# A fused expert MLP and adapter kernel: the order of its front and its drain, and the down projection from f16 parts

## The reference, cut to what matters

```python
# layer 0, expert e = itok_B_0_7[b]
h = gelu(x @ Wi[e] + bi[e])                  # 256 -> 1024
r = h @ Wo[e] + bo[e] + x                    # 1024 -> 256
y = (r - mean) * rsqrt(var + 1e-12) * gamma[e] + beta[e]
# layer 1, domain d = itok_B_0_15[b]
a = gelu(y @ down_W.T + down_b)              # 256 -> 64, the "down projection"
a = a @ expert_W[d].T + expert_b[d] + domain_emb[d]
r = a @ up_W.T + up_b + y                    # 64 -> 256
out = (r - mean) * rsqrt(var + 1e-5) * ln_gamma + ln_beta
```

## Time and profile before

| what | value |
|---|---|
| median of the runs | 487.38 us |
| the profiled execution: time and span | 487.38 us, 485.6 us |
| mean granted TensorE clock | 0.981 |
| PE busy | 457.4 us (94%) |
| DVE, ACT, POOL busy | 341.8, 361.8, 344.0 us (70%, 74%, 71%) |

### The profile page before, as it was taken

The page is one execution under the profiler, slowest core; times in us unless marked ns, Lnnn a source line. Parts: engine busy times, 40 slices in busy tenths (PEclk is TensorE's granted clock), DMA queues, the critical chain, the costliest instruction groups (busy, mean ns, idle before and its releaser), DMA issues.

```text
span 485.6 us, 18802 instructions
## 1 busy us (share of the span) xinstructions
PE 457.4 (94%) x5724; PEld 423.8 (87%) x5725; DVE 341.8 (70%) x910; ACT 361.8 (74%) x1087; POOL 344.0 (71%) x567
## 2 busy tenths in 40 slices
PE   3599999999999999999999999999999999999972
PEld 2388999999999999999999999999999999888861
DVE  7677777877777777777777787777777766665352
ACT  2499777887777877778877788777788777776631
POOL 6043677887778877887788887886788877754465
PEclk9899999999999999999999999999999999999995
DMA  4924333334443333333433443333432222220101
GB/s 106 332 74 106 94 100 101 104 88 102 106 104 97 103 98 93 100 96 102 104 88 95 103 103 98 86 102 99 102 97 65 61 63 62 59 59 24 26 22 32
DMA packets 66809, 44.36 MB, mean 91 GB/s; under 512 B 41538, under 2 KB 58323, under 8 KB 66643
## 3 DMA queue, kind: packets, MB, share of 16 engines
q1 hardware_dynamic: 65744, 43.68, 34.0%
q10 hardware_dynamic: 1026, 0.21, 0.2%
HBM read 35.47 MB, written 8.39 MB: 90 GB/s over the span
## 4 chain that ended last, share of the span: by engine, by line
PE 89%; DVE 3%; issue 2%; POOL 2%; ACT 2%; DMA 0%; POOLq 0%; DVEq 0%
PE p_o L1019 12%; PE p_o L1018 12%; PE p_o L1017 12%; PE p_h L1006 12%; PE p_h L1007 11%; PE p_h L1008 11%; PE p_d L1029 7%; PE p_u L1043 6%; PE p_t L1051 3%; PE p_u L1039 2%; PE p_o L1117 1%; PE p_h L947 1%; DVE W L810 1%; ACT h L639 0%; ACT ctab L591 0%
## 5 line engine op out<-in xcount | busy, mean ns | idle before, releaser
L1006 PE MATMUL p_h<-x_hi,W 128*128 128x128 f16 (+1 forms) x1088 | 183.5, 217 | 3.3 <-issue 3.3
L1007 PE MATMUL p_h<-x_lo,W 128*128 128x128 f16 (+1 forms) x1088 | 183.4, 217 | 0.0
L1008 PE MATMUL p_h<-x_hi,W 128*128 128x128 f16 (+1 forms) x1088 | 183.4, 217 | 0.0
L639 ACT ACTIVATE h<-p_h,bi_tile 128x128 f32<-128x128 f32 (+1 forms) x544 | 148.6, 358 | 0.0
L1019 PE MATMUL p_o<-W,h_lo 128*128 x512 | 139.6, 273 | 0.0
L1018 PE MATMUL p_o<-W,h_hi 128*128 x512 | 139.6, 273 | 0.0
L1017 PE MATMUL p_o<-W,h_hi 128*128 x512 | 139.6, 273 | 0.0
L1006 PEld LDWEIGHTS p_h<-x_hi,W 128*128 x1088 | 105.8, 98 | 8.0 <-issue 6.6
L1007 PEld LDWEIGHTS p_h<-x_lo,W 128*128 x1088 | 105.7, 98 | 2.0
L1008 PEld LDWEIGHTS p_h<-x_hi,W 128*128 x1088 | 105.7, 98 | 0.0
L539 POOL TENSOR_TENSOR rs<-mv,neg_half 128x1 f32<-128x1 f32 x64 | 55.1, 860 | 69.2 <-DVE mv L882 69.2
(11 more groups left out here) (167 smaller groups left out, 825.4 us busy)
## 6 DMA issues: line engine op xcount, KB each, us to landing
stage<-in_w SPq DMA_DIRECT2D x56, 256.0 KB, 2.7
x_nat<-in_x SPq DMA_DIRECT2D x128, 64.0 KB, 2.2
out<-y SPq DMA_DIRECT2D x128, 64.0 KB, 2.0
x_T<-in_xT SPq DMA_DIRECT2D x126, 64.0 KB, 2.2
W<-in_w SPq DMA_DIRECT2D x8, 256.0 KB, 4.4
g_t<-in_gamma SPq DMA_DIRECT2D x1, 1024.0 KB, 7.3
W<-in_expert_W SPq DMA_DIRECT2D x2, 128.0 KB, 2.8
upT<-in_up_W SPq DMA_DIRECT2D x2, 64.0 KB, 2.6
```

The source lines that it names most:

```text
L639: ins = nc.scalar.activation(h[:, c, mine], p_h[parity][:, c, mine], ACT.Gelu, bias=bi_tile[:, parity, n, c:c + 1], scale=1.0 / (XS * WS))
L1006: mm(out, hi, x_hi[:, parity, k, mine], start=(k == 0), stop=False)
L1007: mm(out, hi, x_lo[:, parity, k, mine], start=False, stop=False)
L1008: ins = mm(out, lo, x_hi[:, parity, k, mine], start=False, stop=(k == KD - 1))
```

## The change

Four groups of edits, as the diff has them.

1. **Down projection.** `down_hi` and `down_lo` are f16 parts of 512 times down_W, made once in step 1. ACT writes `yT_hi` = f16(8·gamma·z) (Copy with gamma as scale, no bias); DVE writes `yT_lo` in the new `low_y`, at the end of its step. TensorE does six f16 matmuls in place of two f32 ones. Beta's share, down_W·beta + down_b, is computed per expert in front (`beta_down`) and goes in as the bias of the GELU, whose scale takes the factors out. `gb_tile` has two parities now and three columns instead of four.
2. **Front.** No `ctab` round before step 0; round r stands behind the first product of step r, r = 0 to 3. SP issues four first chunks, then tile 1's x, then the other four. One later weight chunk per step in steps 0 to 3, two in steps 4 and 5. SP's order in the first eight steps has the chunk last. `u_s` is copied before the last four first chunks.
3. **Mixed tiles.** The index table has six entries per step; a step that touches a mixed tile reads all six in one call.
4. **Drain** (steps 64 to 68). The transposes come behind the second product. DVE has an order of its own; for the last four tiles ln_gamma and ln_beta are applied on DVE (`late_gamma`, `late_out`), not on POOL.

```diff
+        down_hi = sb("down_hi", [P, KD, P], f16)
+        down_lo = sb("down_lo", [P, KD, P], f16)
@@ SP
-            for m in FIRST_ORDER:
-                sp.dma_start(first_stage[m], t["w"][bass.ds((expert + m) * P, P), :]).then_inc(first_in[m], 16)
+            load_first(FIRST_ORDER[:4])
             sp.wait_ge(idx_ready, SRC_READY)
             load_turned(indices(sp, IDX_SP + 6, 2, B - 1), 1, 1)
+            load_first(FIRST_ORDER[4:])
@@ the chunks that a step splits
-            if isinstance(i, int) and i < EARLY:
-                return [(2 * i + q, (2 * i + q, 1, 2 * i + q)) for q in range(2)]
+            if isinstance(i, int) and i < LEAD - EARLY:
+                js = [i] if i < 4 else [2 * i - 4, 2 * i - 3]
+                return [(j, (j, 1, j % SLOTS_W)) for j in js]
@@ POOL
-                    need(pool, yT_done, i - 2)
+                    need(pool, a1_done, i - 3)
@@ ACT
+                    for n, mine in tokens(i - 3):
+                        ins = nc.scalar.activation(a1[:, mine], p_d[:, mine], ACT.Gelu,
+                                                   bias=gb_tile[:, 1 - parity, n, KD:KD + 1], scale=1.0 / (YS * DS))
@@
-                            ins = nc.scalar.activation(yT[:, k, mine], turned_z[:, mine], ACT.Identity,
-                                                       bias=gb_tile[:, n, KD + k:KD + k + 1],
-                                                       scale=gb_tile[:, n, k:k + 1])
+                            ins = nc.scalar.activation(yT_hi[:, k, mine], turned_z[:, mine], ACT.Copy,
+                                                       scale=gb_tile[:, parity, n, k:k + 1])
@@ DVE
+                def late_gamma():
+                    dve.wait_ge(mv2_done, i - 3)
+                    v.scalar_tensor_tensor(y[:, parity, :], yg[:, parity, :], mv[:, 1, 0:1], lng[:, :],
+                                           ALU.subtract, ALU.mult).then_inc(yl_done, 1)
+                def late_out():
+                    dve.wait_ge(rs2_done, i - 3)
+                    v.scalar_tensor_tensor(y[:, parity, :], y[:, parity, :], rs[:, 1:2], lnb[:, :],
+                                           ALU.mult, ALU.add).then_inc(y_late, 1)
+                def low_y():
+                    dve.wait_ge(yT_high, i - 1)
+                    for k in range(KD):
+                        for n, mine in tokens(i - 2):
+                            ins = v.scalar_tensor_tensor(yT_lo[:, k, mine], p_t[:, k * P:k * P + P][:, mine],
+                                                         gb_tile[:, parity, n, k:k + 1], yT_hi[:, k, mine],
+                                                         ALU.mult, ALU.subtract)
+                    ins.then_inc(yT_done, 1)
+                if drain(i):
+                    if exists(i - 1):
+                        split_h(i - 1, 1 - parity, 1)
+                    if exists(i - 2):
+                        residual_1()
+                        aggr_1()
+                    if exists(i - 4):
+                        residual_2()
+                        stats_2()
+                        aggr_2()
+                    if exists(i - 2):
+                        normal_1()
+                    if exists(i - 4):
+                        late_gamma()
+                    if exists(i - 3):
+                        low_a()
+                    if exists(i - 4):
+                        late_out()
+                    if exists(i - 2):
+                        low_y()
+                    return
@@ TensorE
-                        ins = mm(p_d[:, 0:P], downT[:, k, :, :], yT[:, k, :], start=(k == 0), stop=(k == KD - 1))
+                        mm(p_d[:, 0:P], down_hi[:, k, :], yT_hi[:, k, :], start=(k == 0), stop=False)
+                        mm(p_d[:, 0:P], down_hi[:, k, :], yT_lo[:, k, :], start=False, stop=False)
+                        ins = mm(p_d[:, 0:P], down_lo[:, k, :], yT_hi[:, k, :], start=False, stop=(k == KD - 1))
@@
+                    for r, top in zip(indices(pe, 6 * i + IDX_PE, 6 if two_places else 4, DOMAIN_TOP),
+                                      2 * [PLACE_TOP] + 2 * [DOMAIN_TOP] + 2 * [PLACE_TOP])]
@@
-                if isinstance(i, int) and i == 0:
-                    pe.wait_ge(u_ready, 1)
-                    pe.wait_ge(idx_ready, TILE_READY)
-                    c_tables(2, [p_t[:, :], p_d[:, :]])
-                if isinstance(i, int) and i == 1:
-                    pe.wait_ge(c_copied, 6)
-                    c_tables(3, [p_t[:, :], p_d[:, :]])
+                for r in rounds(i):
+                    if r == 0:
+                        pe.wait_ge(idx_ready, ALL_READY)
+                    else:
+                        pe.wait_ge(c_copied, 2 * r)
+                    if r == 3:
+                        pe.wait_ge(a1_done, 1)
+                    c_tables(r, table_banks(r))
@@
-                    if j == TR_AT and exists(i - 2):
+                    if j == TR_AT and exists(i - 2) and not drain(i):
                         transpose()
...
+                if drain(i) and exists(i - 2):
+                    transpose()
```

More of the change, by code:

```diff
@@ L98, in build @@
         z1 = sb("z1", [P, D])
-        gb_tile = sb("gb_tile", [P, 2, 2 * KD])
-        yT = sb("yT", [P, KD, P])
+        gb_tile = sb("gb_tile", [P, 2, 2, KD + 1])
+        yT_hi = sb("yT_hi", [P, KD, P], f16)
+        yT_lo = sb("yT_lo", [P, KD, P], f16)
         sel_tile = sb("sel_tile", [P, 4, P], f16)
@@ L326, in h_parts, with rounds, table_banks, drain @@
                     for u in range(2)]
+        def rounds(i):
+            return [i] if isinstance(i, int) and i < 4 else []
+        def table_banks(r):
+            return [(p_t if r < 2 else p_u)[:, :], p_d[:, :]]
+        def drain(i):
+            return isinstance(i, int) and i >= TILES
+        def late(j):
+            return isinstance(j, int) and TILES - 4 <= j < TILES
         def loads(i, parity, each):
@@ L399, in step, with load_chunk @@
             def step(i, parity, four, weights):
-                if weights:
+                def load_chunk():
                     if weights[0] == 0:
@@ L403, in step @@
                     load_later(i + AHEAD, expert[0], weights[0], weights[2])
+                starting = isinstance(i, int) and i < LEAD
+                if weights and not starting:
+                    load_chunk()
                 if exists(i + 2) or exists(i - 5):
@@ L414, in step @@
                     load_natural(b[0:2], i, parity)
+                if weights and starting:
+                    load_chunk()
             run(sp, step, NCH, AHEAD, 2 * LEAD)
@@ L504, in step @@
                 e_third, e_before, _, _, e_next = indices(pool, i + (IDX_EXP - 3), 5, E0 - 1)
-                if exists(i - 5):
+                if exists(i - 5) and not late(i - 5):
                     last = y[:, 1 - parity, :]
@@ L618, in _ @@
                     high_x(0, 0)
+                if n == 4:
+                    act.wait_ge(beta_down, 1)
+                    act.wait_ge(adapter_in, 6 * 16)
+                    nc.scalar.activation(gb_c[:, :, KD:KD + 1], ph_flat[1][:, WCH:WCH + E0].unsqueeze(2), ACT.Identity,
+                                         bias=downb[:, :]).then_inc(downb_ready, 1)
+                    act.wait_ge(u_summed, 1)
+                    nc.scalar.copy(u_s[:, :], ph_flat[1][:, 0:D]).then_inc(u_ready, 1)
                 act.wait_ge(first_in[m], 16)
@@ L625, in _ @@
                                  ACT.Copy, scale=CS).then_inc(c_plain_hi, 1)
-            copy_round(1, both)
-            act.wait_ge(u_summed, 1)
-            nc.scalar.copy(u_s[:, :], p_t[:, D:2 * D]).then_inc(u_ready, 1)
             def gelu(i, parity, half):
@@ L907, in step @@
                     split_h(i, parity, 0)
-                if isinstance(i, int) and i < 2:
-                    low_round(2 + i, [p_t[:, :], p_d[:, :]])
+                for r in rounds(i):
+                    low_round(r, table_banks(r))
+                if exists(i - 2):
+                    low_y()
+                if isinstance(i, int) and i == 1:
+                    dve.wait_ge(down_high, 1)
+                    v.scalar_tensor_tensor(down_lo[:, :, :], down_flat, DS, down_hi[:, :, :], ALU.mult, ALU.subtract)\
+                        .then_inc(down_split, 1)
             run(dve, step, NCH)
@@ L958, in _ @@
             pe.wait_ge(wt_ready, 2)
+            pe.wait_ge(cols_in, 2 * 16)
+            pe.wait_ge(adapter_in, 6 * 16)
+            for k in range(KD):
+                ins = mm(ph_flat[1][:, WCH:WCH + E0], down_flat[:, k, :], gb_in[:, :, KD + k], start=(k == 0),
+                         stop=(k == KD - 1))
+            ins.then_inc(beta_down, 1)
             pe.wait_ge(up_in, 2 * 16)
-            both = [ph_flat[1][:, 0:WCH], ph_flat[1][:, WCH:2 * WCH]]
-            c_tables(0, both)
             pe.wait_ge(embb_ready, 1)
@@ L1055, in up_weights @@
                     return ctab_flat[:, bass.ds(domains[n] + part * D, D)]
```

(12 more changed lines are left out.)

131 lines of the change are left out of this document (83 added, 48 removed).

## The result

The changed kernel takes 472.09 us (median of four runs, 471.92 to 472.45); the kernel before, run beside it, 487.25 us (486.91 to 487.96). The ratio is 0.9688, interval 0.9671 to 0.9705. The forecast was 471.0 in a range of 467.5 to 476.5. Of the forecast saving of 16.4 us, 15.2 came.

The account below looks back on a forecast made before the run. TensorE was taken to bound the steady part, where only what it executes counts. Savings of 10.1 (down projection), 2.8 (mixed tiles), 3.5 (front) and 0 (drain) sum to 16.4: 487.4 - 16.4 = 471.0 us, range 467.5 to 476.5.

Parts of the forecast that it names:

- Down projection, -10.1 forecast: Steps 4 to 64: six f16 matmuls take 0.335 us against 0.50, saving 0.165 a step over 61 steps.
- Rival C: Down projection: loads of the six matmuls don't overlap, so nothing is gained on TensorE; 481 us, chance 0.04.
- Rival B: Steady steps: DVE, ACT or POOL becomes the pace in part, half of the 0.165 lost; 476 us, chance 0.10.
- Rival D: Steady steps: a ring of low_y, residual, h_lo, GELU and yT sets the pace, step 6.9 us; 495 us, chance 0.03.
- Mixed tiles, -2.8 forecast: Four mixed steps: one call of six registers removes the 3.3 us of issue gaps; bounds 1.2 to 3.3 gained.
- Front, -3.5 forecast: Up to step 4: first GELU 4.8 us sooner, partly given back by moved rounds; bounds 1 and 5.5 gained.
- ACT paces steps 0 to 3: Front: ACT has 6.1 to 6.8 us of work in steps 2 and 3, so it sets the pace.
- Rival A: Front: it gives nothing back in net, through TensorE idling, low clock, moved rounds and later chunks; 474.5 us, chance 0.17.
- TensorE's two idle stretches of 1.1 and 1.7 us: Front, after TensorE starts step 0: waits for x of tile 1 (1.1 us) and round 0's low part (1.7).
- Drain, 0 forecast: From tile 63's residual to the last y: losses and gains sum to +0.15 us, bounds -1.5 to +2, taken as 0.
- The residual was to come 1.95 later: Drain: tile 63's residual queues behind tile 62's low_y, which waits for the transposes and ACT's pieces; 1.95 us later.

Follow-up runs that it names:

- r12: The kernel before with only the six-entry index table and one call of six registers in steps touching a mixed tile; 483.71 us, ratio 0.9932.
- r2: The changed kernel with the down projection back in f32 on TensorE, fed by an f32 tile that low_y writes; 482.53 us, ratio 0.9905.
- r9: The changed kernel with low_y's two instructions done twice, the extra pass into a spare tile; 475.49 us, ratio 0.9753.
- r10: The changed kernel with low_y's two instructions done three times, the extra passes into a spare tile; 484.23 us, ratio 0.994.
- r3: The changed kernel with a mixed step's six registers read in three calls (4+1+1) in place of one; 472.7 us, ratio 0.9697.
- r11: The changed kernel with mixed steps' extra registers read two at a time (4+2+2), one of each pair unused; 474.28 us, ratio 0.9735.
- r6: The changed kernel with the loads of gamma and the two layer-norm rows issued behind step 0's loads of x; 470.6 us, ratio 0.9661.
- r4: The changed kernel with the old drain order (drain() and late() false everywhere); 472.21 us, ratio 0.9698.
- r5: The changed kernel with step 64's transposes back inside its second product, the rest of the drain kept; 470.63 us, ratio 0.966.

## Why the prediction was right, and where its terms were off

**Down projection, -10.1 forecast.** Right in mechanism and nearly in size. The pitch of 0.056, the step of 6.50 to 6.51, DVE's 5.4 to 5.5 us a step, the place of low_y in front of the residual and the remaining wait of 0.86 are as forecast. ACT's instruction lost one per-partition operand, and two of them went from 0.81 to 0.63 us: 0.09 each. The steady part gives 9.27 of it over 56 steps, 0.1655 a step. The forecast counted five more steps, the mixed ones, at 0.165 each (0.83); there the edit gives 0.27 (r12 against after) to 0.30 (r2 against after). The forecast took the mixed steps for paced by the matmuls throughout, and they aren't. From the first record of a down projection to the next matmul of another kind it is 0.54 us once and 0.53 three times in r2, and 0.34 in after: 0.77 shorter over steps 60 to 63. But 0.5 of that comes back in the first products of the same steps, where the 361 distances from record to record add up to 11.10 us in after and 10.61 in r2. The largest, where the neighbours are 0.03 apart:
```profile
421.31 0.19 PE L1140 MATMUL p_h<-x_hi,W 128*128 128x64 f16 x1
421.58 0.20 PE L1138 MATMUL p_h<-x_hi,W 128*128 128x64 f16 x1
```
The second record waits for no semaphore, so no other engine holds it. TensorE's sequencer works out addresses there (`second_addresses` and `first_addresses`, L1130 and L1124); that this sets the pace is inferred and not tested. Together -9.6.

Rival C (f16 doesn't overlap) is refuted: here a matmul of such a stream takes 55.9 ns, in the six new ones too. By the Trainium skill, "TensorE: Matmul & The Clock Gate", section "Back-to-back issue gap", it would take about 81 ns. The trace disagrees with that. Rival B is refuted by the step itself (6.51) and by r9, which lays 0.5 us more on DVE at no cost in the steady part. Rival D, a ring through ACT that paces when low_y and its wait pass 1.7 us, did not come, and no run shows such a ring: in after the two take 0.73 (202.63 to 203.36), and in r10 1.55 (203.12 to 204.67), where the step begins to grow because DVE's own work fills it, while ACT still waits.

**Mixed tiles, -2.8 forecast, -3.3 measured (r12): near by luck in part.** The gap was read rightly from the earlier trace rows, its cause only in part. The forecast said "a call costs about 0.6 us of TensorE's sequencer". A call of two registers does take 0.53 to 0.55, but the price is that of the registers and of their place in the table, and not one of a call: r3 makes three calls in a step and loses nothing, and a single call of six takes 0.82 or 1.47. Of the 3.3 us about 1.7 come from reading six registers in one call in place of four, two and two (r11 against after, in the mixed steps). The other 1.6 are left for the table's six entries a step, which r11 has too and the kernel before has not: its call of four takes 0.34 in place of 1.00 in steps 61 and 63. The forecast has no such term. It took 2.8 of a gap of 3.3, and any explanation that removes the gap gives that.

**Front, -3.5 forecast, -2.1 measured (1.0 to 2.5 over the traces).** This is the mis-sized term. The first GELU came at 22.41, as forecast (22.3), 4.68 us before the old one at 27.09. The forecast gave back 1.3 of it; 2.6 went. The starts of the first GELU of steps 1, 2 and 3 say where, after and then before:
```profile
28.87 1.12 ACT L695 ACTIVATE h<-p_h,bi_tile 128x128 f32<-128x128 f32 x4
...
34.17 1.17 ACT L695 ACTIVATE h<-p_h,bi_tile 128x128 f32<-128x128 f32 x4
...
41.46 1.12 ACT L695 ACTIVATE h<-p_h,bi_tile 128x128 f32<-128x128 f32 x4
```
```profile
33.55 1.12 ACT L639 ACTIVATE h<-p_h,bi_tile 128x128 f32<-128x128 f32 x4
...
38.53 1.17 ACT L639 ACTIVATE h<-p_h,bi_tile 128x128 f32<-128x128 f32 x4
...
44.71 1.12 ACT L639 ACTIVATE h<-p_h,bi_tile 128x128 f32<-128x128 f32 x4
```
Step 1: the lead is whole, 4.68. Step 2: 4.36, 0.3 lost to `down_hi`. Step 3: 3.25, another 1.1. Step 2 now holds two copy instructions of a round, and step 3 a wait of 0.99 for the down projection where it was 0.67. Step 4's up projection: 2.08, another 1.2, for step 3's round. So the two rounds that were moved cost 1.1 and 1.2, about what the forecast put for their copies (1.06), and there is no cover. The forecast let ACT's copies be "1.06 more" in both steps yet put the gain between 2.3 and 4.2 and took 3.5; the low end was the right one.

It was wrong too that "ACT paces steps 0 to 3". In step 3 ACT waits, and the chain runs over DVE's low parts to the down projection:
```profile
39.05 0.67 DVE ctab L876
39.73 0.53 DVE yT_lo L980 x2
```
r9 confirms it: with one more pass of low_y its step from the second to the third GELU start is 7.81 us (35.38 to 43.19) against 7.29, so that pass (0.52) is paid there in full. Rival A's loss didn't come, though part of its reasons did: the first product ran at half the rate of the later ones, and both rounds are paid. TensorE's two idle stretches of 1.1 and 1.7 us came out as none and 0.35.

Beside that, ACT waits 1.32 us for x ahead of step 1. In the kernel before it waited 0.77 at this place, but split one chunk of weights more, so the lead stayed whole. There the x tiles were issued at 29.01 and 29.81, when gamma's load had landed; in the changed order they leave behind it. r6 gains 1.4 us by turning the two around.

**Drain, 0 forecast, -0.3 measured.** The residual was to come 1.95 later. Against r4, which has the old order, it comes 1.99 later (8.42 and 6.43 us after step 64's up projection: 456.54 - 448.12 and 454.06 - 447.63), and against the kernel before (469.55 - 463.06) 1.93. The rest of the new drain pays for that, as forecast, and r5 shows what remains when the delay is taken out: 1.8 us.

**Sum.** -9.6, -3.3, -2.1 and -0.3 make -15.3; measured 15.2. The four come from parts of the same two traces, so that they add up proves nothing of its own. r2 and r12 tie the first two to their causes, and r4 and r5 the last. The front's is read from traces: no run moves one of its rounds alone in the old order.

## What to carry to other kernels

When one engine is never idle, price a change of its instruction stream by the pitch of the same form elsewhere in the trace, and price the others only up to the waits that they have (here 1.7 us of DVE's were free, and the step moved only as they were used up, in r10). Work that is moved from before a loop into its first, paced steps kept its full price here; follow the lead over these steps, not at the first one only, and on every engine that the work touches. A gap with no releaser can be the engine's own sequencer: ask the profile for the line of the register loads and add up their durations before a price is put on a call. Where an order of instructions changes at a pipeline's end, look for a waiting instruction that is put ahead of the one on the chain: here it hid 1.8 us in an edit that measured as nothing.

## What the hardware showed that was not expected

**A granted clock of 1.00 beside a half-rate pitch.** In the changed kernel's first product the matmuls start 0.107 us apart, where later it is 0.056. Timeline, then the window with its granted clock (third from the end):
```profile
18.43 0.31 PE L1138 MATMUL p_h<-x_hi,W 128*128 128x128 f16 x1
18.54 0.31 PE L1139 MATMUL p_h<-x_lo,W 128*128 128x128 f16 x1
```
```profile
18.00:22.00 4.00, 3.86 (x37) 3.87 (x38) 3.73 (x7) 4.00 (x11) 0.23 (x1) 1.00 1.02 358
```
The record says full clock (2.4 GHz) and the pitch is the half-rate one (1.2 GHz). It falls to 0.056 at 22.16, after the matmuls had run without a wait since 18.14. In the kernel before pitch and record agree at this stage: 0.107 from 24.48 to 26.61, with 0.50 recorded between 24 and 26 us. Earlier they don't: its eight f32 matmuls of round 0 last 2.04 us at 14.58, with 1.00 recorded between 14 and 16 us, and those of round 1 last 2.08 at 0.50. So near the start of this program the pitch, and not the recorded clock, tells the rate. It cost little here: ACT's splitting of the weights ends at about the time when the first product does, and the first GELU has no wait before it (22.41).

**Reading registers.** A load of registers on TensorE's sequencer takes 0.30 us for one, 0.53 to 0.55 for two, 0.34 or 1.00 for four and 0.82 or 1.47 for six, by its place in the table (what the calls take, under r12). It stays hidden up to 1.1 to 1.3 us a step here, and what goes beyond shows as a gap without a releaser. Why the place matters, no run shows.

**Small loads behind a large one.** With a load of 1 MB, which fills 128 partitions from one set of rows, on its way since 18.91, a tile of 64 KB issued at 22.02 lands after 6.0 us; issued ahead of it, in r6, after 3.8; at 27.50 in the changed kernel, when it has landed, after 2.3. The large load itself takes 8.0 us, and 5.3 in r6.
